# Last cross-attention of a four-block kernel: the transposes of a group are issued ahead of the weighted sums of the group before it

## What is computed

```python
xn = layernorm(x, gm, bm)            # x here is the context
ln = layernorm(latents, gl, bl)      # latents is the normed stream
q = ln @ Wq
kv = concatenate([xn, ln], axis=-2) @ Wkv
k, v = split(kv, 2, axis=-1)         # 8 heads of 64
q, k, v = (heads(q), heads(k), heads(v))
q = q / scale
sim = einsum('bhid,bhjd->bhij', q, k)
sim = sim - max(sim, axis=-1, keepdims=True)
attn = softmax(sim, axis=-1)
out = einsum('bhij,bhjd->bhid', attn, v)
return out.reshape(B, L, H * dh) @ Wout
...
x = x + tanh(g_xattn[3]) * L3_xattn(context, layernorm(x), ...)
x = x + tanh(g_ffn[3]) * L3_ffn(layernorm(x), ...)
```

## Time and profile before

| what | us |
|---|---|
| median of 3 runs | 743.63 |
| the three runs | 743.63, 735.77, 746.27 |
| the profiled execution | 746.65 |
| its span (first to last instruction) | 744.9 |
| TensorE busy | 688.9 (92% of the span) |
| VectorE busy | 560.3 (75%) |
| ScalarE busy | 489.3 (66%) |
| GpSimd busy | 215.0 (29%) |
| first scores of the last attention start at | 549.0 |
| its last projection starts at | 662.7 |

### The profile page before, as it was taken

One profiled execution on the slowest core, in us unless ns is written; L12 is line 12 of the kernel. 1 busy time (PEld: TensorE's weight loads), 2 busy tenths in 40 slices (PEclk: granted clock), 3 DMA queues, 4 the chain that ended last, 5 costly groups with the idle time before them and its releaser, 6 DMA issues.

```text
span 744.9 us, 14725 instructions
## 1 busy us (share of the span) xinstructions
PE 688.9 (92%) x4872; PEld 368.8 (50%) x4872; DVE 560.3 (75%) x1749; ACT 489.3 (66%) x1342; POOL 215.0 (29%) x197
## 2 busy tenths in 40 slices
PE   6999999799999998999699999999979999989997
PEld 3655566466566432333245566655335665563332
DVE  4789898779998578677956999976038888845663
ACT  3778894389996688588857999834666666523201
POOL 2614662371444277336713032331000000000000
PEclk9899999899999989999899999999999999999999
DMA  5786000175000000000001600000000000000500
GB/s 204 158 253 259 1 3 1 33 162 127 3 2 2 2 0 1 0 2 0 0 22 45 128 2 2 2 29 1 0 0 1 1 2 1 0 1 1 227 2 28
DMA packets 20987, 31.81 MB, mean 43 GB/s; under 512 B 1648, under 2 KB 17968, under 8 KB 20272
## 3 DMA queue, kind: packets, MB, share of 16 engines
q1 hardware_dynamic: 20912, 30.86, 14.5%
HBM read 23.22 MB, written 7.63 MB: 41 GB/s over the span
## 4 chain that ended last, share of the span: by engine, by line
PE 69%; DVE 16%; ACT 8%; issue 5%; DMA 1%; POOL 1%; DVEq 0%; ACTq 0%; SPq 0%
PE bank L1137 12%; PE bank L1378 9%; DVE RING L1940 5%; PE bank L1408 4%; PE bank L1251 4%; PE bank L1540 4%; PE bank L1238 4%; DVE RING L1952 4%; PE bank L1327 4%; PE bank L1265 3%; PE bank L1527 3%; PE bank L1388 2%; PE bank L1740 2%; PE bank L1713 2%; PE bank L1158 2%
## 5 line engine op out<-in xcount | busy, mean ns | idle before, releaser
L938 ACT ACTIVATE RING<-RING,NMX 128x256 f32<-128x256 f32 x384 | 190.9, 500 | 25.8 <-DVE NMX L1940 24.1
L1940 DVE CUSTOM_DVE_ANT_0 RING<-bank,ADJM 128x256 f32<-128x256 f32 x384 | 145.5, 418 | 19.6 <-PE bank L1327 16.6
L1378 PE MATMUL bank<-W,RING 128*128 128x128 f32 x768 | 118.5, 287 | 5.4 <-ACT RING L950 5.1
L1378 PEld LDWEIGHTS bank<-W,RING 128*128 128x128 f32 x768 | 83.6, 144 | 52.9 <-ACT RING L938 41.5
L1952 DVE COPY RING<-bank 128x512 f32<-128x512 f32 x144 | 98.6, 686 | 5.6 <-PE bank L1378 5.2
L618 POOL TENSOR_TENSOR SUMS<-SUMS,small 128x8 f32<-128x8 f32 x36 | 59.2, 1644 | 127.0 <-ACT RING L938 127.0
L576 POOL TENSOR_TENSOR small<-small 128x2 f32<-128x2 f32 (+2 forms) x17 | 19.4, 1138 | 215.0 <-DVE small L1798 214.9
L938 ACT ACTIVATION_READ_ACCUMULATOR RING<-RING,NMX 128x1 f32 x384 | 72.8, 189 | 0.0
L852 ACT ACTIVATE RING<-bank,NMX 128x512 f32<-128x512 f32 x64 | 43.4, 684 | 39.1 <-DVE NMX L1882 29.2
L1882 DVE TENSOR_REDUCE NMX<-bank 128x1 f32<-128x512 f32 x64 | 39.8, 683 | 31.4 <-PE bank L1238 31.3
L1540 PE MATMUL bank<-ARENA,W 64*128 64x512 f32 x180 | 60.5, 669 | 2.3 <-DVE ARENA L2168 1.9
(11 more groups left out here) (265 smaller groups left out, 1241.3 us busy)
## 6 DMA issues: line engine op xcount, KB each, us to landing
ARENA<-scratch SPq DMA_DIRECT2D x12, 384.0 KB, 7.0
ARENA<-wrows SPq DMA_DIRECT2D x8, 512.0 KB, 7.5
scratch<-ARENA SPq DMA_DIRECT2D x18, 192.0 KB, 2.8
W<-in_weights SPq DMA_DIRECT2D x1, 2564.0 KB, 22.7
ARENA<-scratch SPq DMA_DIRECT2D x12, 192.0 KB, 3.7
scratch<-ARENA SPq DMA_DIRECT2D x18, 128.0 KB, 6.7
W<-in_weights SPq DMA_DIRECT2D x2, 1024.0 KB, 14.3
W<-in_weights SPq DMA_DIRECT2D x1, 1905.5 KB, 15.4
```

What stands on the lines that cost most here:

```text
L938: nc.scalar.activation(P_OF(n)[:, q * S:(q + 1) * S], S_OF(n)[:, q, :], ACT.Exp, bias=NMX[:, 2 * t + q:2 * t + q + 1], scale=-1.0, accum_o ...
L1378: mm = nc.tensor.transpose(bk[:, o:o + P], P_OF(n)[:, i:i + P], ident)
L1940: nc.vector.tensor_tensor_reduce(out=S_OF(n)[:, q, :], in0=SBANK(n)[:, q * S:(q + 1) * S], in1=ADJM[:, b, q, :], scale=-1.0, scalar=BIG, o ...
```

## The change

In TensorE's program alone, the two parts of a turn behind the scores change places: the transposes of group G - 1 are issued first, the weighted sums of group G - 2 behind them. Their instructions, waits and signals are the same ones. No other engine's program changes.

```diff
@@ latents() of TensorE, in for G in range(LG + 2): @@
                             nc.tensor.matmul(bank[j][:, :], QT3[r:r + 64, g, q:q + P], KT3[r:r + 64, g, b, :],
                                              start=True, stop=True).then_inc(l_s, 1)
+                    if 1 <= G < LG + 1:
+                        E = G - 1
+                        for j in range(4):
+                            u = 4 * E + j
+                            pe.wait_ge(l_nm, u + 1)
+                            if u >= 3:
+
+                                m = u - 3
+                                pe.wait_ge(l_te if m % 2 else l_to, m // 4 * 2 + m % 4 // 2 + 1)
+                            for k in range(4):
+                                mm = nc.tensor.transpose(bank[4 + u % 3][:, k * P:(k + 1) * P],
+                                                         LP_OF(u)[:, k * P:(k + 1) * P], ident)
+                            mm.then_inc(l_t, 1)
                     if G >= 2:
                         H = G - 2
                         b, g = H // 4, H % 4
...
                         mm.then_inc(l_pv, 1)
-                    if 1 <= G < LG + 1:
-                        E = G - 1
-                        for j in range(4):
-                            u = 4 * E + j
-                            pe.wait_ge(l_nm, u + 1)
-                            if u >= 3:
-
-                                m = u - 3
-                                pe.wait_ge(l_te if m % 2 else l_to, m // 4 * 2 + m % 4 // 2 + 1)
-                            for k in range(4):
-                                mm = nc.tensor.transpose(bank[4 + u % 3][:, k * P:(k + 1) * P],
-                                                         LP_OF(u)[:, k * P:(k + 1) * P], ident)
-                            mm.then_inc(l_t, 1)
                     if G == LG + 1:
                         turn(XN, 0, 4, rk, s_fk)
```

## The result

| | before | changed |
|---|---|---|
| median of 4 runs, us | 744.95 | 753.83 |
| lowest and highest | 735.77, 753.55 | 747.29, 758.62 |
| the profiled execution | 746.65 | 755.48 |
| its span | 744.9 | 753.7 |
| first scores to last projection of the attention, in the profile | 113.71 | 124.40 |

The ratio of the changed kernel to the one before is 1.0133, with a 95% interval from 1.0067 to 1.0199. The median of before now has a fourth run, 753.55. The forecast was 1.6% and a verdict within 2%.

The account below looks back on a forecast made before the run. TensorE was taken as full, VectorE having only 0.35 us to spare. Turns 7.52 and 3.36, turn 2 0.77 and tail 0.15 make 11.8 us on a 743.63 median: 755.4, 1.6% slower, range 749 to 764.

Parts of the forecast that it names:

- regular turn: Attention loop, turn without a projection: 6.90 us against 5.96, +0.94, as the last unit waits for VectorE's copy.
- projection turn: Turns 6, 10 and 14, where the projection reads ScalarE's copy of the weighted sums: 9.42 us against 8.30, +1.12.
- turns 3 to 13, added: Eleven turns from turn 3 to turn 14: 8 x 0.94 = 7.52 plus 3 x 1.12 = 3.36.
- turn 2, added: First turn with all parts, its scores at half clock: scores of turn 3 at 567.66 against 566.89, +0.77.
- tail, added: From turn 14's scores to weighted sums 15: 21.0 us against 20.85, +0.15; 1 to 2 worse at half clock.
- from the last unit to what stands behind it: TensorE's last transposed unit to the next work: 0.59 us from a regular turn, 0.69 from turn 1.
- The lower end, 6.84: Regular turn summed from 1.16, 2.40, 0.81, 0.59 and 1.88: +0.88 a turn.
- The upper end, 6.96: Regular turn summed with turn 1's links, 1.16, 2.40, 0.83, 0.69 and 1.88: +1.00 a turn.
- The clock rival: Attention loop: idle pieces of 0.9 a turn drop TensorE's clock; twelve such turns give 785 us; chance 0.10.
- The ScalarE rival: Attention loop: ScalarE, with 0.42 to spare, becomes last link; copies 0.7 later give about 760 us; chance 0.08.
- No stall: Attention loop: first copy starts by 2.68 after the scores, turns stay 5.96, tail -2.7, kernel 740.9 us; chance 0.06.

Follow-up runs that it names:

- the doubled copy: The changed kernel with ScalarE's copy of the last transposed unit done twice in each turn; one run, 755.60 us.
- the copy after two maxima: The changed kernel with VectorE's copy of a group's first transposed unit between the second and third maximum; 739.77 us, 0.9994 of before.
- the fourth unit behind: The changed kernel with the fourth unit's transposes issued behind the weighted sums on TensorE; 736.45 us, 0.9909 of before.
- the copy after three maxima: The changed kernel with VectorE's copy of the first transposed unit between the third and fourth maximum; one run, 746.68 us.
- the last two kernels: Changed kernel with fourth unit behind weighted sums and first copy after two maxima, 738.46 us; the same with layer-norm statistics moved to turn 16, 735.94 us.
- both edits: The changed kernel with the fourth unit behind the weighted sums and VectorE's first copy after two maxima; 738.46 us, 0.9924 of before.

## Why the prediction was right, point by point

The terms of the sum, as forecast and as the profile has them:

| term | forecast | measured |
|---|---|---|
| regular turn | 6.90 (6.84 to 6.96) | 6.82 |
| projection turn | 9.42 | 9.36 (579.32 to 588.68) |
| turns 3 to 13, added | 10.88 | 10.12 (82.66 - 72.54) |
| turn 2, added | 0.77 | 0.79 (8.18 against 7.39) |
| turns 0 and 1, added | 0 | -0.15 (10.35 against 10.50) |
| tail, added | 0.15 | -0.07 |
| sum | 11.8 | 10.69 |

*The mechanism* is the one forecast, link by link. In turn 4 of the changed kernel it is scores to maxima 1.16, maxima to copy 2.40, copy to the fourth unit's weights 0.80, to the weighted sums 0.58, to the next scores 1.88: 6.82. The forecast had 1.16, 2.40, 0.81, 0.59 and 1.88. The term that was mis-sized is one link, from the last unit to what stands behind it. The lower end, 6.84, took 0.59 from a regular turn and was right (0.58). The upper end, 6.96, took 0.69 from turn 1, and over those 0.69 the granted clock was already down to 0.76; the changed kernel's turn 1 needs 0.55 for the same link, at 1.00. The middle, 6.90, is 0.08 above a measured turn, and the projection turns' 9.42 is 0.06 above. Turns 3 to 13 are 0.76 of the 1.1 by which the sum was too high; the same link is most of the 0.15 in turns 0 and 1, and the 0.64 taken for it in the tail, where 0.55 and 0.58 were measured, is part of the tail's 0.22. A row at a lower granted clock is no price for a piece that is forecast at the full one.

*The clock rival* (0.10) did not come: the granted clock is 1.00 from turn 3 to turn 13 with an idle piece of 0.94 in every turn. The trace of before had shown 7 us with 6.00 of work at 1.00, and that reading held. The rule of the Trainium skill ("TensorE: Matmul & The Clock Gate", section "A second HAM failure mode: psum-queue depth-cycling"), that short idles between groups make the clock go back and forth, would have made this rival come true. In this loop, with its idle pieces of 0.94 and its granted clock of 1.00, the trace does not show it.

*The ScalarE rival* (0.08) did not come either, and its reasoning was faulty. "It has 0.42 to spare" was the time until its first exponential can start, but that exponential is not what the chain waits for. The run with the doubled copy used up more than 0.42, though the exponential came only 0.11 later by it, and no turn grew. A slack is to be counted to the point where somebody on the chain waits, not to the engine's own next instruction.

*No stall* (0.06) did not come: every regular turn has the stall. The run with the copy after two maxima shows that the condition this rival named, a copy that starts 2.68 behind the scores, was the right one: there it does, and the turn is 5.96, at which the prediction had put it. What it said of the tail came true only for the slow weighted sums, which took 1.95. It also let the two waits for ScalarE's transposed units go, and had the kernel 2.7 faster; in that run the tail, to the last weighted sums, still waits 1.41, 1.06 and 1.46 and is 19.93 against 20.85, and the whole attention is 1.4 shorter than before.

*The tail* gave back what it cost, as forecast, and its steps came where they were put: the maxima of turn 15 at 8.45 (forecast 8.48), weighted sums 13 at 12.23 (12.34), the first transpose of turn 16 at 15.25 (15.40), weighted sums 15 at 20.78 (21.0). But the two lengths compared are not alike. The kernel before has half clock in its 20.85: its weighted sums of group 14 took 2.99, in the changed kernel 1.95. The forecast took its own tail all at full clock, gave no reason for it, and kept 1 to 2 more for half clock in the range. That the clock held is what its even sum rests on, and so far it was luck: with 1.54 more of idle time in the tail than before, a clock as before would have made it longer by about that much, and in the run with ScalarE's copy twice the clock did fall, at the tail's last weighted sums.

*The time.* 755.4 was forecast for the median and 753.83 measured; 10.69 added to the 743.63 known then would have been 754.3.

## What to carry to other kernels

When a full engine's work is reordered, look for the instruction in it that waits for a buffer which its own group has just filled, and ask what stands between the two: here 1.88 us of weighted sums ahead of the transposes gave VectorE the time for its maxima before the copy behind them was due, and moving them uncovered 0.94 a turn at no change in busy time. There are two cures, and both were measured: put the covering work between the third and the fourth user of three buffers (0.9% faster than before), or let the engine that frees the buffer do so ahead of work for which nobody waits yet (back to even). Of the two, the first has the shorter attention in the trace, by 4.2. It gains 3.0 in turns 3 to 13, of which 2.1 are the projection turns (7.79 against 8.49), since ScalarE has the weighted sums in time, and 2.2 in the tail, and loses 1.0 in turns 0 to 2. The intervals of the two whole kernels still touch (0.9859 to 0.9959, 0.9938 to 1.0049).

## What the runs showed of the hardware

What TensorE's clock did behind an idle piece showed on one spot of the program. Ahead of the scores of turn 2, TensorE waits in turn 1 for VectorE's copy: 2.42 in the changed kernel, 1.22 with the copy after two maxima. The scores behind it ran at a granted clock of 0.53 in the first, 1.00 in the second. The two rows, first the changed kernel, then the one with the early copy (columns as in the earlier trace rows):

```profile
557.49:561.11 3.62, 3.62 (x10) 1.18 (x9) 2.96 (x6) 1.51 (x5) 0.00 (x0) 0.53 0.02 5
```

```profile
548.84:551.32 2.48, 2.48 (x10) 0.97 (x9) 2.13 (x6) 2.35 (x6) 0.00 (x0) 1.00 0.00 0
```

The other traces agree at this spot: behind 2.42 the clock was 0.55 in the kernel before and with ScalarE's copy twice, and 0.67 with the fourth unit behind; behind 1.82, with the copy after three maxima, 0.57; behind 1.23, in the last two kernels, 1.00. So a copy that came 1.2 earlier shortened turn 2 as well, and the first scores to those of turn 3 by 1.7 (16.83 against 18.53) instead of 1.2. The tail of the kernel with the doubled copy is the same from the other side: an idle piece of 2.09 instead of 1.46, and the weighted sums behind it took 3.48 instead of 1.95. Idle pieces of 0.94 in each of eleven turns cost no clock at all. The length of the last idle piece does not decide by itself, though. With both edits, 1.90 of idle time in the tail left the clock at 1.00, where 1.82 in turn 1 of another kernel did not; and in the kernel before, the weighted sums that took 2.99, at 0.63, stood behind a piece of only 0.96, itself 0.6 behind one of 1.69. Each of these is one execution; what tells the cases apart stays open.
